# Pass 0 of a graph kernel: the one-hot of the low source bits in pairs of equal elements, and the placing of message pieces walked in adjacent pairs

## The reference

```
x_j = node_features[col]                               # one source node's 16 features per edge
m = einsum('ei,ej,ijh->eh', x_j, edge_attr_e3nn, W_msg_tp) * norm_msg_tp
m = silu(m);  m = m @ W_msg_lin * norm_lin             # 16 numbers per edge
agg = segment_sum(m, row, num_segments=n_nodes)        # summed into the node `row` of the edge
u = einsum('ni,nh,ihk->nk', node_features, agg, W_upd_tp) * norm_upd_tp
return node_features + silu(u) @ W_upd_lin * norm_lin
```

## Time and profile before

| | |
|---|---|
| median of 3 runs | 9480.41 us |
| span of the profiled execution, first to last instruction | 9468.5 us |
| pass 0, first scatter to the last | 339.9 to 2597.0 us of the span |
| stage N0 | to about 2847 us |
| TensorE, VectorE, ScalarE, GpSimd busy over the span | 90%, 74%, 39%, 56% |
| mean granted TensorE clock | 0.922 |

### The profile page before, as it was taken

The page is one execution under the profiler, slowest core; times in us unless marked ns, Lnnn a source line. Parts: engine busy times, 40 slices in busy tenths (PEclk is TensorE's granted clock), DMA queues, the critical chain, the costliest instruction groups (busy, mean ns, idle before and its releaser), DMA issues.

```text
span 9468.5 us, 206077 instructions
## 1 busy us (share of the span) xinstructions
PE 8528.1 (90%) x70979; PEld 6184.9 (65%) x70979; DVE 6983.9 (74%) x13558; ACT 3699.8 (39%) x10806; POOL 5317.9 (56%) x4703
## 2 busy tenths in 40 slices
PE   1599999999985889998689999998999998999998
PEld 0366666666625777777567777776777776777776
DVE  2488889999842222222178888887999998999998
ACT  5245444444330000100045555554555554555554
POOL 0588878888770000000067666644877776877775
PEclk9999999999965888888689999998999998999998
DMA  8733333333309767667933332222222222222221
GB/s 300 241 92 100 104 116 105 105 105 104 87 1 379 270 235 282 245 235 267 390 66 70 70 69 69 70 68 47 53 54 54 54 53 45 53 54 54 53 54 39
DMA packets 869344, 1162.78 MB, mean 123 GB/s; under 512 B 269991, under 2 KB 751539, under 8 KB 868359
## 3 DMA queue, kind: packets, MB, share of 16 engines
q1 hardware_dynamic: 674852, 1078.23, 34.4%
q0 software_dynamic: 150336, 28.94, 4.1%
q10 hardware_dynamic: 43426, 45.70, 1.5%
HBM read 1018.19 MB, written 133.22 MB: 122 GB/s over the span
## 4 chain that ended last, share of the span: by engine, by line
PE 51%; DVE 25%; DMA 7%; POOL 6%; SPq 5%; issue 4%; ACT 1%; DVEq 0%; ACTq 0%
PE ps L840 17%; PE ps L919 9%; DVE msg L2020 7%; POOL arena L666 6%; PE ps L720 6%; DMA arena<-adj 5%; DVE arena L2013 4%; DVE dinv L2013 4%; PE ps L798 4%; SPq L585 3%; PE ps L857 3%; PE ps L709 3%; DVE invdeg L1469 2%; DVE dinv L1469 2%; PE ps L805 2%
## 5 line engine op out<-in xcount | busy, mean ns | idle before, releaser
L666 POOL DMA_INDIRECT arena<-tab,x_all x3030 | 3302.6, 1090 | 3279.2 <-DMA tab<-stage 2135.8
L684 POOL DMA_INDIRECT adj<-acc x1616 | 1961.7, 1214 | 557.9 <-issue 470.0
L919 PE MATMUL ps<-arena 128*128 128x192 bf16 (+1 forms) x16464 | 1171.9, 234 | 172.4 <-DMA arena<-adj 171.5
L919 PEld LDWEIGHTS ps<-arena 128*128 128x128 bf16 x16464 | 1121.4, 103 | 231.2 <-DMA arena<-adj 200.3
L1115 ACT ACTIVATE wide<-ps,not_all 128x256 bf16<-128x256 f32 x1616 | 739.4, 483 | 1195.6 <-PE ps L805 1195.6
L720 PE MATMUL ps<-dinv,acc 128*128 128x384 bf16 x5454 | 967.7, 333 | 46.1 <-DVE acc L1501 45.6
L1287 ACT ACTIVATE arena<-w_iota,rel 128x128 f32<-128x128 f32 x3232 | 988.8, 388 | 13.1
L720 PE MATMUL ps<-invdeg,acc 128*128 128x384 bf16 x5454 | 989.6, 338 | 2.8 <-issue 2.8
L720 PEld LDWEIGHTS ps<-dinv,acc 128*128 128x128 bf16 x5454 | 536.1, 102 | 430.2 <-issue 127.6
L720 PEld LDWEIGHTS ps<-invdeg,acc 128*128 128x128 bf16 x5454 | 543.3, 104 | 404.9 <-issue 110.2
L1638 DVE TENSOR_TENSOR arena<-hot_a,threes 128x1024 bf16<-128x1024 bf16 x606 | 738.3, 1218 | 0.0
(11 more groups left out here) (321 smaller groups left out, 14373.2 us busy)
## 6 DMA issues: line engine op xcount, KB each, us to landing
arena<-adj SPq DMA_DIRECT2D x588, 896.0 KB, 6.9
x_all<-src_parts SPq DMA_DIRECT2D x606, 192.0 KB, 3.2
arena<-rels SPq DMA_DIRECT2D x202, 512.0 KB
arena<-tab SPq DMA_DIRECT2D x1616, 64.0 KB
adj<-zero SPq DMA_DIRECT2D x28, 3136.0 KB, 27.8
arena<-rT SPq DMA_DIRECT2D x404, 128.0 KB
arena<-tab,x_all POOLq DMA_INDIRECT x3030, 2.4
adj<-acc POOLq DMA_INDIRECT x1616
```

What stands on the lines that cost most here:

```text
L666: pool.indirect_dma_start(G[b][:, u, :], None, TABLE[PHASES[p]], bass.IndirectOffsetOnAxis(ap=idx[:, t:t + 1], axis=0)).then_inc(gathered[ ...
L684: pool.indirect_dma_start(adj_cells, bass.IndirectOffsetOnAxis(ap=pair[:, t, 0:1], axis=0), pair16[:, t, 2:3], None).then_inc(celled[g], 16)
L919: last = mm(ps[:, 2 * par + u // 2, u % 2 * W:(u % 2 + 1) * W], ring[i][:, s, u * P:(u + 1) * P], rows[:, j * SC + s, :, :].rearrange("p k ...
```

## The change

`hot_a` gets a fourth dimension of 2: each of its values stands twice, side by side (128 instead of 64 bf16 per partition). Its one-hot is made by the same instruction, with twice the results. `place` reads and writes the same values as before, but walks the 16 features as 8 pairs: the innermost run of `hot_a` is now a pair of adjacent equal elements, stepped over 8 times in place, where before it was one element read 16 times.

```diff
-        hot_a = sb("hot_a", [P, HT, A8], bf16)
+        hot_a = sb("hot_a", [P, HT, A8, 2], bf16)
...
             def place(h, i):
-                tt(placed[h][:, i, :, :, :], hot_a[:, :, :].unsqueeze(3).to_broadcast([P, HT, A8, 16]),
-                   threes[h][:, :, i, :].unsqueeze(2).to_broadcast([P, HT, A8, 16]), ALU.mult).then_inc(v.sem, 1)
+                tt(placed[h][:, i, :, :, :].rearrange("p u a (f c) -> p u a f c", c=2),
+                   hot_a[:, :, :, :].unsqueeze(3).to_broadcast([P, HT, A8, 8, 2]),
+                   threes[h][:, :, i, :].rearrange("p u (f c) -> p u f c", c=2).unsqueeze(2)
+                   .to_broadcast([P, HT, A8, 8, 2]), ALU.mult).then_inc(v.sem, 1)
...
-                tt(hot_a[:, :, :], w["iota"][:, 0:A8].unsqueeze(1).to_broadcast([P, HT, A8]),
-                   src_a[:, ds(k * HT, HT)].unsqueeze(2).to_broadcast([P, HT, A8]), ALU.is_equal).then_inc(v.sem, 1)
+                tt(hot_a[:, :, :, :], w["iota"][:, 0:A8].unsqueeze(1).unsqueeze(3).to_broadcast([P, HT, A8, 2]),
+                   src_a[:, ds(k * HT, HT)].unsqueeze(2).unsqueeze(3).to_broadcast([P, HT, A8, 2]), ALU.is_equal
+                   ).then_inc(v.sem, 1)
```

## The result

The changed kernel takes 9431.71 us (median of 6 runs, 9423.87 to 9442.59) where the kernel before takes 9472.14 us (6 runs, 9460.06 to 9489.0; the first three are those behind the 9480.41 us): a ratio of 0.996, 95% interval 0.9948 to 0.9971. The forecast was 9450 us with a range from 9438: right in sign, 18 us too high, and 6 us outside the range.

What follows compares the result with a forecast made beforehand. TensorE was taken to bound pass 0's quiet part, so only its waits, the degree rounds, small lateness and clock gain: 30.1 us off 9468.5 gives span 9438.4, median 9450.3 us. Own range 9442 to 9459; eight in ten 9438 to 9473.

Steps and rivals of the forecast that it cites:

- Rate of `place`: VectorE's `place` with bf16 pairs makes two results per cycle: 690 ns instead of 1218; `hot_a` grows from 216 to 282 ns.
- Where TensorE waits: TensorE's waits for `place` in pass 0 fall from 31.6 us (13 times) to about 11 us (6 times).
- quiet pitch: Time per batch in pass 0's quiet part, 145 batches, where TensorE is the bound: stays 10.825 us, gain zero.
- small lateness: Some 36 batches with the extra count but no table load, each 0.083 us over the quiet pitch: 3.0 us gained.
- product's wait for `expand`: VectorE, done earlier in quiet batches, waits for `expand` before the product: from 13 us in pass 0 to about 200.
- Sum: All gains in pass 0 added: 10.9 + 9.6 + 1.6 + 3.0 + 5.0 = 30.1 us, all arriving at the end.
- seven waits at table loads: Seven TensorE waits for `place` of 1.55 to 1.63 us, with ScalarE's extra count and table load, fall to about zero: 10.9 us.
- six longer waits and the degree rounds: Six longer TensorE waits each lose 1.6 us (9.6 us); the degree rounds behind PLACED(11) start 1.6 us earlier.
- clock: Three falls of TensorE's granted clock behind pauses of 1.55 us vanish: 3 x 1.66 = 5.0 us, bounds 0 and 7.8.
- excess of 2.0 us a batch: GpSimd's issues lengthened beside `place`; excess falls to about 1.1 us, saving some 180 us, so GpSimd ends near 2650.
- Rival 2: GpSimd's issues stay at 1214 ns and its end at 2829.4 holds pass 1's table loads: 9463 to 9464 us; chance 0.07.

Runs made afterwards that it cites:

- pairs_unused: Changed kernel with `hot_a` still in pairs, but `place` reading one element of each pair 16 times; 9481.51 us, ratio 1.0 to the kernel before on chip C.
- after_again: The changed kernel, unedited, timed again on chip C: 9449.80 us, ratio 0.9967 to the kernel before.
- after_no_cells: Changed kernel with GpSimd's adjacency writes left out for all batches but the first; 9447.44 us, ratio 0.9968 to the kernel before on chip C.
- no_cells_again: The kernel of after_no_cells once more, on chip F: 9445.8 us, ratio 0.9972 to the kernel before.
- before_no_cells: Kernel before with GpSimd's adjacency writes left out for all batches but the first; 9476.9 us, ratio 0.9996 to the kernel before on chip C.
- same_after: The changed kernel, unedited, on chip B: 11909.5 us, ratio 1.0328 to the kernel before there.

## Why the prediction was right and wrong

*Rate of `place`.* 690 forecast, 685 ns measured; `hot_a` 282 and 283. pairs_unused shows that the walk in pairs is the cause.

*Where TensorE waits.* 31.6 to about 11 us was forecast, 11.1 measured, 5 times; the difference of 20.5 is the sum's 10.9 + 9.6. The quiet pitch stays 10.825, and the small lateness is gone. The product's wait for `expand` came to 160 us, forecast as 200; some of the rest went to the wait before `rest` (204 to 301 us in all).

*Sum.* 30.1 forecast for pass 0; 31.2, 31.4 and, without GpSimd's writes, 30.4 us measured. That it came so near is in part luck, as the starts and lengths of the 202 scatters in the two first profiles show, matched batch by batch:

| term | forecast | measured |
|---|---|---|
| seven waits at table loads | 10.9 | 11.1 |
| six longer waits and the degree rounds | 9.6 + 1.6 | 7.2 |
| small lateness | 3.0 | 3.0 |
| clock | 5.0 | 9.9 |

The first of the six waits lies ahead of the first scatter, outside pass 0 as timed here, and the gain at the second doesn't reach the scatter behind it: the third scatter starts only 0.7 us sooner, and so did the first. The clock gave twice its term and more than its bound of 7.8: besides the three falls and that behind the square root, two more were shorter (at 383.95 and 519.85). In after_again it is 9.0 us. The link between pauses and falls, which the prediction called uncertain, is borne out as far as profiles can: behind 530 us none of the four of the change with unpaced writes (after, after_again, after_no_cells, no_cells_again) has a scatter above 8.5 us, and the three quick ones of the old `place` (before, before_no_cells, pairs_unused) have two to four.

*GpSimd.* A step that failed in size: the excess of 2.0 us a batch "for 3.65 us of `place`" was scaled with the time of the places. It goes more nearly by the square of each one's length: 246 ns an issue fell to 79, not to 140, a factor of 0.32, and (685/1218) squared is 0.32. At 8 x (1.047 + 0.30) = 10.8 us a batch it no longer falls behind TensorE's 10.83, and its last write ends 5 us behind the last scatter, at 2570, not 2650. Since it wasn't the bound either way, this cost the forecast nothing on a quick chip.

*The range.* This is the step of the prediction that failed: all its terms were mechanisms, and to the wandering of the medians it gave 6 us. The changed kernel's median is 9431.71 us in one timing and 9449.80 in the next, 18 us apart; the kernel before's is 9480.41 over its first three runs, from which the forecast was reckoned, and 9472.14 with three more. Of the 16.4 us by which the span came out under the forecast's 9438.4, only 1.8 lie in or ahead of pass 0; 14.6 lie in stages that the change doesn't touch. These don't repeat: from L614 to the end the changed kernel took 11.6 us less than before in the first profile, and 12.6 us more in after_again (6633.9 against 6621.3). The low end should have stood some 15 us lower. As a ratio the forecast was 0.9968; measured were 0.996 (0.9948 to 0.9971), and 0.9967 on C.

*What it didn't see at all.* Rival 2 asked only whether GpSimd ends too late. On three of the chips it is GpSimd's speed that hurts: the time that the change gives it is paid for by TensorE. This is shown for the changed kernel on B, and by its variants on D and E. The trace of before had no row of this, since on that chip TensorE doesn't dribble. What makes a chip of that kind, and by which way GpSimd's writes reach TensorE, stays open: the waits are ones that nothing in the profile ends, and the part that a lower granted clock plays (0.82 to 0.90 while GpSimd writes) wasn't separated from them. SyncE is slowed along with TensorE (its eight loads L599 of one batch take 5.96 and 6.81 us at 1501 and 1510 us in same_after, 4.10 and 3.97 at 601 and 1497 in before), so it isn't TensorE's alone; what the two share, no run shows.

## What to carry to other kernels

A small operand that is broadcast along the innermost axis costs the fast rate; kept twice side by side and read in pairs it gave 685 in place of 1218 ns. What that is worth is not the busy time saved (324 us) but the bound engine's waits for the result, term by term (31 us): list them, see which a part of the gain already covers, and leave out those ahead of the stage or behind a load that stays late.

A faster engine also sets another one free. Here GpSimd's transfers became denser, which was harmless in the first timing and on C, and cost 3.3% on B; variants of the change cost 1 to 4% on D and E. Time a change of this kind on more than one chip before believing a gain of 0.4%, and give the range of a forecast the spread of the medians.

## What the runs showed of the hardware

- Chips, or their state in one hour, differ in kind: the same kernel takes 9475 to 9481, 11005, 11520 and 11536 us, and the difference lies in the stretches in which GpSimd issues an indirect transfer one after the other (pass 0 and passes 7 to 9). In one execution TensorE went from 596 busy of 680 us at a granted clock of 0.90 to 281 of 281 at 1.00 when GpSimd stopped.
- On such a chip 0.17 us more between two writes of GpSimd (1.44 in place of 1.27) took pass 0 from 3390 us (chip B) to 2743 us (chip D, whose kernel before is as fast as B's).
- An indirect issue that meets a place takes longer. What a place standing alone costs GpSimd went by its length squared (0.65 us for 1.218 us, 0.22 for 0.685); two halves of 0.684 us back to back cost 0.58, more than twice the square's 0.21.
- A VectorE product of two bf16 inputs, one read as a pair 8 times over, made 1024 results in 685 ns.
